# Local attention products as 64x64 halves, second-bank copies and one table call on ScalarE, bias table in four loads

## The reference, cut to what matters

```
h = layernorm(groupnorm(x)); h = roll(h, (3, 3))
h = windows of 7x7 positions            # 16 * 8 * 8 windows, L = 49 tokens each
q, k, v = split(h @ qkv_w.T + qkv_b)    # 4 heads of 8 channels
bias = pe_table[:, idx].reshape(4, 49, 49)   # idx from the 13x13 relative offsets
o = softmax(q @ k.T / sqrt(8) + bias) @ v
o = o @ out_w.T + out_b                 # back to 56x56
y = gelu(layernorm(o) @ mlp_w1.T + mlp_b1) @ mlp_w2.T + mlp_b2
x = x + y; t = layernorm(x)
```

## Time and profile before

| what | value |
|---|---|
| median of 3 runs | 2917.95 us (2916.13 to 2920.89) |
| the profiled execution, own time | 2920.42 us |
| its span (first to last instruction) | 2918.6 us |
| setup, until the first `center_window` | 0 to 80 us |
| local attention | 80 to 797 us, 21.3 us a chunk in its middle |
| preparation | 797 to 888 us |
| global attention and experts | 888 to 2918.6 us |
| busy over the span | PE 94%, DVE 79%, ACT 70%, POOL 21% |

### The profile page before, as it was taken

One profiled execution on the slowest core, in us unless ns is written; L12 is line 12 of the kernel. 1 busy time (PEld: TensorE's weight loads), 2 busy tenths in 40 slices (PEclk: granted clock), 3 DMA queues, 4 the chain that ended last, 5 costly groups with the idle time before them and its releaser, 6 DMA issues.

```text
span 2918.6 us, 60087 instructions
## 1 busy us (share of the span) xinstructions
PE 2752.7 (94%) x24969; PEld 1299.2 (45%) x24969; DVE 2308.7 (79%) x3007; ACT 2049.6 (70%) x3863; POOL 619.1 (21%) x506
## 2 busy tenths in 40 slices
PE   3799999999788999999999999999999999999987
PEld 2455555555452344344343444434434344344337
DVE  4799999999568787877878878878788787787843
ACT  3587777878654777777777777777777777777762
POOL 0456656565400110100101101011010010110100
PEclk8799999999997999999999999999999999999997
DMA  4000000000183011010110100101101011010003
GB/s 96 1 24 19 24 19 23 20 18 24 34 318 76 1 23 23 1 23 1 23 24 1 23 18 7 23 1 24 23 1 23 1 23 23 1 23 1 1 1 90
DMA packets 93923, 82.12 MB, mean 28 GB/s; under 512 B 62453, under 2 KB 83542, under 8 KB 92630
## 3 DMA queue, kind: packets, MB, share of 16 engines
q1 hardware_dynamic: 92085, 78.26, 10.3%
q10 hardware_dynamic: 1568, 0.04, 0.1%
HBM read 39.57 MB, written 32.11 MB: 25 GB/s over the span
## 4 chain that ended last, share of the span: by engine, by line
PE 76%; DVE 16%; ACT 3%; issue 3%; ACTq 1%; DMA 1%; POOLq 0%; POOL 0%; SPq 0%; DVEq 0%
PE ps L1685 20%; PE ps L1658 19%; PE ps L1708 19%; DVE arena L1116 3%; PE ps L1718 3%; DVE arena L1157 3%; DVE arena L1109 2%; DVE arena L1124 2%; PE ps L1670 2%; PE ps L1493 2%; DVE arena L1137 2%; ACT arena L884 1%; PE ps L1763 1%; PE ps L1512 1%; PE ps L1524 1%
## 5 line engine op out<-in xcount | busy, mean ns | idle before, releaser
L1272 DVE TENSOR_REDUCE arena<-ps 128x2 f32<-128x896 f32 (+1 forms) x1408 | 1455.1, 1079 | 353.6 <-PE ps L1658 353.5
L904 ACT ACTIVATE arena<-ps 128x512 f32<-128x512 f32 (+1 forms) x2464 | 1268.5, 603 | 347.0 <-PE ps L1685 333.6
L1685 PE MATMUL ps<-arena 97*128 97x512 f16 x2800 | 818.1, 356 | 10.5 <-ACT arena L904 1.2
L1658 PE MATMUL ps<-arena 96*128 96x448 f16 x2800 | 771.6, 357 | 11.4 <-DVE arena L1262 8.6
L1708 PE MATMUL ps<-arena 128*32 128x512 f32 (+2 forms) x7328 | 666.6, 456 | 0.7 <-DVE arena L1294 0.7
L1685 PEld LDWEIGHTS ps<-arena 97*128 97x128 f16 x2800 | 250.9, 98 | 440.5 <-ACT arena L904 181.9
L1708 PEld LDWEIGHTS ps<-arena 128*32 128x32 f32 x7328 | 237.9, 109 | 406.8 <-ACT arena L904 200.7
L629 POOL TENSOR_TENSOR tok<-arena,tok 128x128 f32<-128x128 f32 (+1 forms) x112 | 47.4, 423 | 1540.6 <-DVE arena L1294 1540.6
L1658 PEld LDWEIGHTS ps<-arena 96*128 96x128 f16 x2800 | 226.4, 99 | 287.2 <-DVE arena L1272 101.9
L574 POOL TENSOR_TENSOR arena<-arena 113x784 f32<-113x784 f32 x128 | 192.5, 1504 | 204.5 <-DVE arena L1127 204.5
L569 POOL TENSOR_TENSOR arena<-arena 113x784 f32<-113x784 f32 x128 | 192.3, 1502 | 82.5 <-DVE arena L1116 78.9
(11 more groups left out here) (185 smaller groups left out, 2586.5 us busy)
## 6 DMA issues: line engine op xcount, KB each, us to landing
arena<-qk_scratch SPq DMA_DIRECT2D x96, 196.0 KB, 4.1
qk_scratch<-arena SPq DMA_DIRECT2D x16, 448.0 KB, 4.9
arena<-ximg SPq DMA_DIRECT2D x16, 400.0 KB, 7.5
arena<-in_x SPq DMA_DIRECT2D x4, 1568.0 KB, 10.1
xa_scratch<-arena SPq DMA_DIRECT2D x32, 196.0 KB, 1.9
res_scratch<-arena SPq DMA_DIRECT2D x32, 196.0 KB, 2.1
arena<-xa_scratch SPq DMA_DIRECT2D x4, 1568.0 KB, 8.6
arena<-res_scratch SPq DMA_DIRECT2D x4, 1568.0 KB, 11.6
```

Of the source, the lines that this page charges most:

```text
L904: act.activation(pk[0:rows, x % DEPTH, QC * m:QC * m + n], ps[0:rows, w % SB, 0:n], ACT.Exp, scale=float(C) ** -0.5).then_inc(att["exp"], 1)
L1272: dve.tensor_reduce(mxp[0:rows, p, 2 * u:2 * u + k], ps[0:rows, at_:at_ + k, 0:KN], AX_X, ALU.max)\
L1658: last = pe.matmul(ps[:, MB + 2 * (j % 2) + n % 2, 0:KN], q2[p][0:96, T * t:T * t + T], k2[p][0:96, KN * m:KN * m + KN], start=True, stop= ...
L1685: last = pe.matmul(ps[:, bank, at_ % QC:at_ % QC + chunk_cols(c)], k2[p][0:97, T * t:T * t + T], q2[p][0:97, QC * c:QC * c + chunk_cols(c) ...
```

## The change

Six edits, all in setup and local attention:

1. The bias table: four loads (one a head) instead of 49. Each brings 49 rows of 85 consecutive table entries; `relb` is taken out of them by one VectorE copy with a four-dimensional pattern. `relr` grows from 196 to 364 elements a partition.
2. `variance`, `out_projection`, `center_window` and the four products for `gnc` are each issued as two products of 64 rows and 64 columns. The variances use the two quadrants on the diagonal (rows 0 to 63 into partitions 0 to 63, 64 to 127 into 64 to 127), the others the two off it, so the image pairs change places after `center_window` and change back in `out_projection`. The matrices are block diagonal by image, so the sums are the same. Both halves of a product write the same PSUM bank, in different partitions.
3. `probs_b` is ScalarE's for all four units; VectorE has none.
4. The order of VectorE's stream: `sums(1)` behind `normalize(.,2)` and `values_copy(0)`, `sums(2)` behind both normalizations, `keys` at the end of the loop, followed by `sums(3)`.
5. The order of TensorE's stream: `center_window` right behind `variance(1)`; `values(2)` between the two projections; both `mlp_out` calls together, behind `scores(1)`.
6. The order of ScalarE's and GpSimd's streams, with the one `log_and_exp` call now between `weighted_copy(2)` and `exponentials(0)`.

The helpers that change:

```diff
-            for qy in range(WS):
-                for qx in range(WS):
-                    p = WS * qy + qx
-                    act.dma_start(relr[p:p + 1, :, :].rearrange("p h (y x) -> p h y x", x=WS),
-                                  tab[:, qy:qy + WS, qx:qx + WS].rearrange("h y (o x) -> o h y x", o=1))\
-                       .then_inc(s_bias, 16)
+            for h in range(NH):
+                act.dma_start(relr[0:L, h, 0:RUN],
+                              bass.AP(tab.tensor, tab.offset + SIDE * SIDE * h, [[SIDE, WS], [1, WS], [1, RUN]]))\
+                   .then_inc(s_bias, 16)
...
-            step(dve.tensor_copy(relb[:, :, :], relr[:, :, ::-1]))
+            step(dve.tensor_copy(relb[:, :, :].rearrange("p h (y x) -> p h y x", x=WS),
+                                 relr[:, :, :].rearrange("p h (y x) -> p h y x", x=SIDE)[:, :, ::-1, 0:WS][:, :, :, ::-1]))
...
-                pe.matmul(ps[:, ZB, 0:CT], cv("mean"), sq[:, :], start=True, stop=True).then_inc(ln[k]["var"], 1)
+                for h in range(2):
+                    r = slice(64 * h, 64 * h + 64)
+                    last = pe.matmul(ps[r, ZB, 0:CT], cv("mean")[r, r], sq[r, :], start=True, stop=True)
+                last.then_inc(ln[k]["var"], 1)
...
-                pe.matmul(ps[:, XB, 0:CT], wp[:, 256:384], oc[:, :], start=True, stop=True).then_inc(ln[1]["center"], 1)
+                for h in range(2):
+                    r, to = slice(64 * h, 64 * h + 64), 64 * (1 - h)
+                    last = pe.matmul(ps[to:to + 64, XB, 0:CT], wp[r, 256 + 64 * h:320 + 64 * h], oc[r, :], start=True, stop=True)
+                last.then_inc(ln[1]["center"], 1)
```

More of the change, by code:

```diff
@@ L779, in _ @@
             for k in range(-3, CHUNKS):
[L780 to L812, removed]
                 if on(k):
@@ L1167, in skip_connection @@
                    .then_inc(conv["t1"], 1)
-            for k in range(-2, CHUNKS):
+            for k in range(-3, CHUNKS):
                 if on(k + 1):
[L1171 to L1189, removed]
+                    dve.wait_ge(conv["exp"], 4 * k + 8)
                     sums(3)
@@ L1225, in _ @@
                     values_copy(0)
+                    dve.wait_ge(conv["exp"], 4 * k + 10)
+                    sums(1)
+                    dve.wait_ge(conv["score"], 4 * k + 12)
                     bias(3)
@@ L1228, in _ @@
                     maxima(3)
-                    dve.wait_ge(conv["ptrans"], 8 * k + 18)
-                    probs_b(0)
+                    dve.wait_ge(conv["vprod"], 4 * k + 10)
+                    values_copy(1)
+                if on(k + 3):
+                    dve.wait_ge(ln[0]["rstd"], k + 4)
+                    normalize(k + 3, 0)
+                if on(k + 1):
+                    dve.wait_ge(ln[1]["rstd"], k + 2)
+                    normalize(k + 1, 1)
+                if on(k + 2):
+                    sums(2)
+                    dve.wait_ge(conv["vprod"], 4 * k + 11)
+                    values_copy(2)
+                if on(k + 3):
+                    dve.wait_ge(conv["qk"], 2 * k + 8)
+                    keys(k + 3)
             def low_part(g, n, i):
@@ L1620, in _ @@
                 if on(k + 2):
-                    pe.wait_ge(conv["bias"], 4 * k + 11)
-                    scores(3)
                     values(k + 2, 0)
+                    pe.wait_ge(conv["prob"], 4 * k + 9)
+                    transposes(0)
                 if on(k + 1):
@@ L1631, in _ @@
                 if on(k + 2):
-                    pe.wait_ge(conv["prob"], 4 * k + 9)
-                    transposes(0)
-                    pe.wait_ge(conv["vcopy"], 4 * k + 9)
-                    values(k + 2, 1)
+                    pe.wait_ge(conv["bias"], 4 * k + 11)
+                    scores(3)
                 if on(k + 3):
@@ new lines, in _ @@
+                if on(k + 2):
+                    pe.wait_ge(conv["prob"], 4 * k + 11)
+                    transposes(2)
+                if on(k + 3):
+                    pe.wait_ge(conv["kz"], k + 4)
+                    pe.wait_ge(conv["qz"], k + 4)
+                    scores(0)
+                if on(k + 1):
+                    pe.wait_ge(conv["gelu"], 4 * k + 6)
+                    hidden_pair(2)
+                if on(k + 2):
+                    pe.wait_ge(conv["oc"], 4 * k + 10)
+                    weighted_values(2)
@@ new lines, in _ @@
+                if on(k + 3):
+                    pe.wait_ge(conv["bias"], 4 * k + 13)
+                    scores(1)
+                if on(k + 1):
+                    mlp_out((0, 1))
+                    pe.wait_ge(conv["gelu"], 4 * k + 8)
+                    mlp_out((2, 3))
+                if on(k + 2):
+                    pe.wait_ge(conv["prob"], 4 * k + 12)
+                    transposes(3)
+                    pe.wait_ge(conv["oc"], 4 * k + 11)
+                    values(k + 2, 3)
@@ L1647, in _ @@
+                if on(k + 1):
+                    pe.wait_ge(conv["t1"], k + 2)
+                    center_sum(k + 1)
+                if on(k + 3):
+                    pe.wait_ge(conv["bias"], 4 * k + 14)
+                    scores(2)
+                if on(k + 2):
+                    pe.wait_ge(conv["pcopy_a"], 4 * k + 12)
+                    pe.wait_ge(conv["vcopy"], 4 * k + 12)
+                    weighted_values(3)
             pe.wait_ge(ln[2]["norm"], CHUNKS)
```

157 lines of the change are left out of this document (78 added, 79 removed).

## The result

The changed kernel runs in 2871.64 us (median of 4 runs, 2866.55 to 2874.15) against 2919.42 for the kernel before (4 runs): a ratio of 0.9832, 95% interval 0.9816 to 0.9848. That is 48 us faster; 45 were forecast.

The account below looks back on a forecast made before the run. Setup was taken as bound by a chain of waits, local attention by TensorE and VectorE. Setup -13.6 and local attention -31 gave -44.6 us, from 2917.95 to 2873.3; range 2852 to 2902.

Parts of the forecast that it names:

- SyncE's list is late once ScalarE is free: Setup: SyncE's 43 small loads, 0.44 us apart, end at 22.8; input group 2 then starts, a gain of 14.5 us.
- two queues taking turns: Setup: SyncE's small loads were 0.64 us apart because its starts alternate with ScalarE's; freed, the pace would be 0.34 to 0.46.
- The eight `gnc` products cost 0.9 us: Setup: four `gnc` products become eight on the chain of waits, costing 0.9 us more, between nothing and 1.87.
- VectorE's work falls to 18.78: Local attention: VectorE loses two copies of 0.54 us a chunk, so its work falls from 19.86 to 18.78 us.
- TensorE needs 19.7 or less: Local attention: halves running beside other products save 0.6 and 0.3 us a chunk from TensorE's 20.55.
- step 4 of the walk: Local attention: `skip` waits for all of `mlp_out`, done at 9.5; wait 0, or 0.6 if the four products do not overlap.
- A gain needs both to shrink: Local attention: TensorE (20.55 us busy) and VectorE (19.86) both bind the 21.32 us period, so both must do less.
- TensorE's waits are 0.2 us: Local attention before the change: TensorE's timeline was read as holding waits of only 0.2 us.
- The walk: Local attention: seven steps through the new orders sum VectorE's waits to 1.45 us, giving a period of 20.25, say 20.3.
- Times 31: Local attention: a gain of 1.0 us in each of 31 periods between first and last `keys`, -31 us, bounds -12 and -50.
- The rival of halves in turn: Local attention: halves writing one PSUM bank run one after the other, period 24.3 us, 2997 us in all; chance 0.07.
- The rival of useless orders: Local attention: ScalarE's delays eat VectorE's saving, period stays 21.3 and only setup gains, 2904 us; chance 0.14.

Follow-up runs that it names:

- the 28 loads: The changed kernel with the bias table in 28 loads of 7 rows each instead of four: 2871.11 us, one run.
- the 49: The changed kernel with the bias table in 49 loads again, all else kept: 2880.22 us, ratio 0.9862 to the kernel before.
- the experiment: The changed kernel with `mlp_out(0, 1)` back behind `hidden_pair(2)`, apart from `mlp_out(2, 3)`: 2889.81 us, ratio 0.9892 to the kernel before.

## Why the prediction was right

The forecast was 2873 with 44.6 us of gain; the medians gave 47.8. Both mechanisms came as forecast: group 2 starts earlier, and both engines near the limit have less to do. That the number is so close is partly luck: in the profiles setup gained 12.9 where I had 13.6, local attention 37.4 where I had 31, and within each errors of opposite sign cancel.

- *SyncE's list is late once ScalarE is free.* Right. I took a pace of 0.44; it is 0.465 once the table loads are over, and 0.76 beside them. The list ends at 25.2 instead of 22.8, and the start of group 2 gains 12.1 us instead of 14.5. The reason I gave, two queues taking turns, is refuted by the 28 loads in the form that I gave it. The 0.52 and 0.32 that I read as a slip don't show turns either: the same load of `wvb` takes 0.33 in the changed kernel, less than its neighbours, with ScalarE starting nothing. By the rule of the Trainium skill, "DMA: Bandwidth & Descriptors", section "Issuing engines are not separate DMA queues", the gain of the list would have been 5.6; the 28 loads agree with it, the 49 do not (0.66 against 0.465 with nothing else changed).
- *The eight `gnc` products cost 0.9 us.* Wrong in sign: 1.87 fell to 1.01, a gain of 0.86. So setup gained 12.9 in the profiles: 12.1 and 0.86, where I had 14.5 less 0.9.
- *VectorE's work falls to 18.78.* 18.96 measured; `normalize(0)` now takes 0.63 and `normalize(2)` 0.57 instead of 0.53 and 0.50.
- *TensorE needs 19.7 or less.* 19.30. The term that was mis-sized is `mlp_out`: I had its overlap in step 4 of the walk as a time, but not in this sum, nor its full worth. Four products cost 0.80 from start to start where two had cost 0.78, and the experiment puts 0.63 us a chunk on it, half of the whole gain. `variance(1)` with `center_window` saved 0.75, not 0.6. On the other side, a cost stood at nothing: with `values(2)` between them the two projections cost 0.86 and 0.95 from start to start, where they had cost 0.76 and 0.66.
- *"A gain needs both to shrink", and "TensorE's waits are 0.2 us".* Both are readings that the rows don't bear. The copies alone gave 0.38 us a chunk with TensorE's work unchanged. And TensorE's period also held a wait of 0.40 for `values_copy(1)`: in the old orders it waited on VectorE, which is why the halves alone gave nothing.
- *The walk.* Waits forecast and measured: before `keys` 0 and 0.16, `bias(0)` 0.1 and 0, `bias(1)` 0.35 and 0.17, `skip` 0 and 0, `normalize(2)` 0.5 and 0.44. `sums(1)` and `normalize(0)` were to wait 0.3 and 0.2 and waited less than 0.1 each. The saved 0.81 did come back in pieces, but smaller ones: period 20.03, not 20.3, and 37.4 us between first and last `keys`, not 31. Times 31 was too simple: 29 periods gained 1.29 each, the first two 0.16 together.
- *The rival of halves in turn* is refuted: `variance` writes bank ZB from two row groups, four instructions in 0.88 us, and in turn they would need 1.5. The Trainium skill, "TensorEngine Tiling (Array Packing)", section "Restrictions and Gotchas", has it that different row tiles cannot use one PSUM bank at a time. Here they do, in different partitions of it, at nearly full pace (0.80 us from start to start, a full product 0.76); same partitions of one bank were not tried.
- *The rival of useless orders* was asked wrongly. The orders alone are worth 0.12 us, near the nothing that it said; but the halves, worth 0.00 in the old orders, are worth 0.36 in the new ones, and 0.80 with the copies on ScalarE.

## What to carry to other kernels

When two engines are both near the limit and meet in fixed orders, an edit's worth is not its own: the same halves were worth 0.00, 0.36 and 0.80 us a chunk, by what else had been changed. Before dropping an edit that measures as nothing, ask which engine's wait it shortens and whether that wait ends last. Ask too what the shortened engine itself waits for: here `center_window` stood behind a VectorE instruction, so its halves had nothing to run beside. Products that use a part of the array gain when they stand next to others that use the rest: halves on the same quadrants as their neighbour gave 0.05 us, on the free quadrants 0.80.

## What the runs showed of the hardware

- A start of a transfer on SyncE took 0.42 us for small loads, and 0.62 while ScalarE started loads of 28 runs of 28 bytes each (median 0.63); beside loads of 7 runs of 340 bytes (median 0.32) it stayed 0.42, beside 49 such runs in one load (0.77) it was 0.74. So it was the form of the loads and not the number of starts that went with the slower starts on the other queue; number and size of the runs were not varied apart.
- Loads of 1 KB started by 26 us landed at 35.1 when two loads of 1.6 MB had been started before them on the same queue.
- Two row groups writing one PSUM bank in different partitions ran side by side: four instructions of 392 columns in 0.88 us, where two of a full product took 0.93.
- Starting the loads of the bias table took ScalarE 33.0 us as 49 loads, 10.1 as 28 and 3.8 as four, although the 28 and the four bring 340 entries a partition and the 49 only 196.
